# When GpSimd computes its low halves and powers, and when the row maxima and LayerNorm 2 are transposed, in a fused attention and FFN layer

## The reference

```python
x = x + attention(layernorm(x), W_qkv, W_out)
x = x + ffn(layernorm(x), U1, V1, b1, U2, V2, b2)

# attention: 32 query heads, 16 key/value heads (each shared by 2 query heads), head size 64
scores = q @ k.T / 8 + slope[head] * (key - query); causal mask; softmax; @ v; @ W_out
# ffn, rank 64:  gelu_tanh((x @ U1) @ V1 + b1) -> @ U2 -> @ V2 + b2
# layernorm: (x - mean) / sqrt(var + 1e-5)
```

## Time and profile before

| | |
|---|---|
| time, median of 3 runs | 2876.21 us (2874.03 to 2881.04) |
| profiled execution: time / span | 2881.05 us / 2879.3 us |
| mean granted clock of PE | 0.989 |
| busy, share of the span | PE 93%, ACT 76%, POOL 70%, DVE 69% |
| a MID body | 173.7 us |
| chain that ended last | PE 71%, ACT 8%, DVE 7%, issue 7%, POOL 5%, DMA 1% |

### The profile page before, as it was taken

How to read it: one execution, slowest core, us unless ns; L and a number is a source line. 1 busy time by engine, 2 the same in 40 slices (tenths; PEclk the granted TensorE clock), 3 DMA queues, 4 the chain that set the end, 5 groups by cost and what they waited for, 6 DMA issues and landing times.

```text
span 2879.3 us, 83610 instructions
## 1 busy us (share of the span) xinstructions
PE 2680.9 (93%) x31112; PEld 1834.4 (64%) x31112; DVE 1992.4 (69%) x6731; ACT 2184.7 (76%) x3892; POOL 2011.7 (70%) x1816
## 2 busy tenths in 40 slices
PE   4999999999999999999999999999999999999986
PEld 1566666766666666666766667666666766667663
DVE  6767676776766767676776776767677676767753
ACT  3777878778787777878778787777878778787782
POOL 1667777777777767777677777777777677777783
PEclk8999999999999999999999999999999999999996
DMA  6444443444434344343544434344343444435420
GB/s 170 96 100 88 94 90 79 104 91 91 89 87 99 82 97 88 87 97 78 105 90 93 89 84 101 85 94 87 88 99 81 98 91 91 92 77 105 87 61 20
DMA packets 495146, 260.82 MB, mean 91 GB/s; under 512 B 317962, under 2 KB 493066, under 8 KB 494474
## 3 DMA queue, kind: packets, MB, share of 16 engines
q1 hardware_dynamic: 494740, 255.47, 40.8%
HBM read 27.73 MB, written 8.39 MB: 13 GB/s over the span
## 4 chain that ended last, share of the span: by engine, by line
PE 71%; ACT 8%; DVE 7%; issue 7%; POOL 5%; DMA 1%; SPq 0%; DVEq 0%; ACTq 0%; POOLq 0%
PE proj L450 31%; PE scores L450 17%; PE o_acc L450 13%; PE max_scores L450 4%; PE ffn_acc L450 4%; ACT h_f L830 2%; POOL p_lo L1090 2%; DVE max_scores L930 2%; ACT p_hi L700 2%; POOL o_hi_lo L1098 2%; ACT p_f L741 2%; ACT L741 1%; DVE h_hi L1022 1%; DMA o_t<-in_L_attn_W_out 1%; POOL h_lo L1118 1%
## 5 line engine op out<-in xcount | busy, mean ns | idle before, releaser
L1090 POOL TENSOR_TENSOR p_lo<-p_f,p_hi 128x512 f16<-128x512 f32 x1280 | 1474.4, 1159 | 564.6 <-ACT p_hi L700 564.4
L741 ACT ACTIVATE p_f<-scores 128x512 f32<-128x512 f32 x1280 | 755.6, 590 | 130.0 <-PE scores L450 126.2
L700 ACT ACTIVATE p_hi<-p_f 128x512 f16<-128x512 f32 x1280 | 800.4, 625 | 14.8
L930 DVE CUSTOM_DVE_ANT_0 max_scores<-max_scores,causal 128x384 f32<-128x384 f32 (+3 forms) x1184 | 563.3, 507 | 268.7 <-PE max_scores L450 257.7
L450 PE MATMUL scores<-q_hi_lo,k_lo_hi 128*128 128x512 f16 (+3 forms) x2048 | 614.2, 300 | 0.2 <-ACT p_f L741 0.2
L450 PE MATMUL scores<-q_hi_aug,k_hi_aug 128*128 128x512 f16 (+3 forms) x2048 | 586.5, 299 | 0.0
L450 PE MATMUL o_acc<-v_hi_one,p_lo 128*128 128x65 f16 x5120 | 518.9, 195 | 42.9 <-POOL p_lo L1090 39.9
L450 PEld LDWEIGHTS o_acc<-v_hi_one,p_lo 128*128 128x128 f16 x5120 | 471.1, 98 | 90.7 <-POOL p_lo L1090 63.2
L450 PE MATMUL o_acc<-v_hi_one,p_hi 128*128 128x65 f16 x5120 | 518.3, 194 | 0.0
L450 PE MATMUL o_acc<-v_lo,p_hi 128*128 128x64 f16 x5120 | 517.9, 193 | 0.0
L450 PEld LDWEIGHTS o_acc<-v_lo,p_hi 128*128 128x128 f16 x5120 | 468.7, 99 | 37.8
(11 more groups left out here) (108 smaller groups left out, 4680.8 us busy)
## 6 DMA issues: line engine op xcount, KB each, us to landing
q_hi_aug<-q_pair_hi SPq DMA_DIRECT2D x512, 64.0 KB, 2.0
q_hi_lo<-q_pair_hi SPq DMA_DIRECT2D x512, 64.0 KB, 2.0
q_hi_lo<-q_pair_lo SPq DMA_DIRECT2D x512, 64.0 KB, 2.0
k_hi_aug<-k_pair_hi SPq DMA_DIRECT2D x256, 64.0 KB, 2.0
k_lo_hi<-k_pair_hi SPq DMA_DIRECT2D x256, 64.0 KB, 2.0
k_lo_hi<-k_pair_lo SPq DMA_DIRECT2D x256, 64.0 KB, 2.0
x_rows<-in_L_attn_inputs SPq DMA_DIRECT2D x17, 512.0 KB, 4.0
x_acc<-in_L_attn_inputs SPq DMA_DIRECT2D x64, 128.0 KB, 2.3
```

The costliest lines, as they stand in the source:

```text
L700: return nc.scalar.activation(out_ap, in_ap, ACT.Copy, scale=scale)
L741: nc.scalar.activation(p_f[:, k % 3, :], score_bank[k % 2][:, :], ACT.Exp).then_inc(exp_done, 1)
L930: last = nc.vector.tensor_tensor_reduce(out=bank, in0=bank, in1=causal[:, (T - 1 - qt) * P:S], scale=1.0, scalar=-3e38, op0=ALU.add, op1=A ...
L1090: nc.gpsimd.tensor_tensor(p_lo[:, slot, n, :], p_f[:, k % 3, :], p_hi[:, slot, n, :], ALU.subtract).then_inc(lo_p, 1)
```

## The change

It moves instructions and adds or removes none of the computation:

- POOL: `low_p` of the stage before now stands ahead of `o_lo` at the start of every stage. `power1` moves from the end of stage 7 to (8, 2), behind that segment's `low_p`. LayerNorm 2's powers move from (8..11, 4) to (9..12, 0), behind `low_p` and `o_lo`.
- The maxima are transposed in segment 2 of stages 2, 6, 10 and 14, not in segment 1. ACT's and DVE's splits of them follow the same table.
- LayerNorm 2: normalising goes from segment 1 to 2, transposing from 2 to 3 of stages 9 to 12. On PE the transposes now stand behind `attend(s, 1)`. DVE's low half of the transposed tile moves to segment 3 with them, and on DVE it stands ahead of that segment's `normalise`.
- DVE's `neg_mean_rstd` goes from (8, 2) to (8, 4).
- `projection_order()` reads the same tables, so the banks of all uses between these places rotate differently.

```diff
-MAX_SEG, K_SEG, V_SEG, O_SEG = 1, 0, 4, 4
+MAX_SEG, K_SEG, V_SEG, O_SEG = 2, 0, 4, 4
...
-VE1_AT, NMR1_AT = (7, 4), (8, 2)
+VE1_AT, RS1_AT, NMR1_AT = (7, 4), (8, 2), (8, 4)
...
-RSTD2_AT = {(8 + t, 4): t for t in range(T)}
-LN2_AT = {(9 + t, 1): t for t in range(T)}
-LN2_T_AT = {(9 + t, 2): t for t in range(T)}
+RSTD2_AT = {(9 + t, 0): t for t in range(T)}
+LN2_AT = {(9 + t, 2): t for t in range(T)}
+LN2_T_AT = {(9 + t, 3): t for t in range(T)}
...
-                            if (s, n) in LN2_T_AT:
-                                transpose_x2(LN2_T_AT[s, n])
...
                         if n in (1, 3) and in_stage(mode, s, ATT + 1):
                             attend(s, n // 2)
+                        if (s, n) in LN2_T_AT and mode != FIRST:
+                            transpose_x2(LN2_T_AT[s, n])
...
+                        if n > 0 and in_stage(mode, s, ATT):
+                            low_p(SEG * (i * KV + s - ATT) + n - 1, s % 2, n - 1, SEG * s + n - 1)
+                        if n == 0 and in_stage(mode, s, ATT + 1):
+                            low_p(SEG * (i * KV + s - ATT) - 1, (s - 1) % 2, SEG - 1, (SEG * s - 1) % (SEG * KV))
                         if n == 0 and in_stage(mode, s, ATT + 2):
                             slot = (s - ATT - 2) % 2
                             pool.wait_ge(hi_o, at(i * KV + s - ATT - 1))
                             nc.gpsimd.tensor_tensor(o_hl[:, slot, 1, :], o_f[:, slot, :, :].rearrange("p t c -> p (t c)"),
                                                     o_hl[:, slot, 0, :], ALU.subtract).then_inc(lo_o, 1)
-                        if n > 0 and in_stage(mode, s, ATT):
-                            low_p(SEG * (i * KV + s - ATT) + n - 1, s % 2, n - 1, SEG * s + n - 1)
-                        if n == 0 and in_stage(mode, s, ATT + 1):
-                            low_p(SEG * (i * KV + s - ATT) - 1, (s - 1) % 2, SEG - 1, (SEG * s - 1) % (SEG * KV))
+                        if (s, n) == RS1_AT and mode != LAST:
+                            power1(i + 1)
...
-                    if s == 7 and mode != LAST:
-                        power1(i + 1)
```

## The result

The changed kernel takes 2882.95 us (median of 13 runs, 2881.08 to 2887.88), the kernel before beside it 2878.0 us (13 runs, 2874.03 to 2881.04). The ratio is 1.0022, interval 1.0013 to 1.0030: 5 to 6 us slower, less than the 0.3% that I called measurable, but clear of 1 by its interval. I had forecast 7 us faster.

What follows compares the result with a forecast made beforehand. PE, busy 93% of the span, bounds the kernel, so its waits are lost time. Gains of 44 and 4.6 us against losses of 39 and 2 us gave about -7 us: 2869 us from 2876.2, range 2838 to 2895.

Steps and rivals of the forecast that it cites:

- The four gains of a MID body: PE waits removed in stages 8, 9, 10 and 2: 1.22, 0.67, 0.82 and 0.22 us, 44 us over 15 bodies.
- k copies at (6, 0) and (8, 0), 0.8 each: Stages 5 and 7: later `o_lo` delays SP's k copies past PE's need, 1.6 us a body together.
- Stages 1 and 3, 0.15 each: k copies behind `o_lo` on SP, late only where an issue or landing is slow: 0.15 us in each stage.
- What is added: Cost step: later `o_lo` holds SP's queue and maxima land later, 2.6 us a body, 39 us, and 2 us once.
- Maxima in segment 2: Stage 6's maxima have nothing in hand before (7, 0): 0.4 us a body; stages 10 and 14 have more in hand.
- the `o_t` transposes: Those needed by output projections of stages 4 and 12, delayed behind later `o_lo` on SP: 0.1 us each.
- FIRST, 2 us: Scores of (7, 0) in the FIRST body wait for the maxima's transpose, now behind a q projection: 2 us, once.
- LAST, 4.6 us: `o_lo` leaves the chain, POOL's work of 6.95 us then limits: 0.65 us a stage over about 7 stages gained.
- A: Rival: only the gains, since SP's copies are not late; 2829 us, chance 0.15.
- B: Rival: SP's queue takes more than is won, at k copies before (6, 0) and (8, 0); 2895 us, chance 0.18.
- C: Rival: `x2n` waits for POOL at the shared port pair, 0.8 us a body in stage 10; 2881 us, chance 0.06.
- D: Rival: ACT's late `p_hi` keeps `attend` waiting in stages 8 and 9, gain about 1 us; 2883 us, chance 0.06.

Runs made afterwards that it cites:

- Experiments one: Kernel before with only `o_lo` moved behind `low_p` on GpSimd; powers, banks and transposes unmoved: 2895.0 us, ratio 1.0053.
- two: Kernel before with only both kinds of LayerNorm powers moved, behind `o_lo`, which stays ahead of `low_p`: 2843.2 us, ratio 0.9882.
- three: Kernel before with only the maxima transposed in segment 2 and LayerNorm 2's subtraction and transpose one segment later: 2873.6 us, ratio 0.9984.
- Experiment four: Changed kernel with `o_lo` back ahead of `low_p`, all else as changed: 2842.0 us, ratio 0.9875.
- experiment five: Changed kernel with the 512 KB load of the next batch's rows issued in stage 2, not stage 1 (`X_LOAD = 2`): 2884.6 us, ratio 1.0019.
- experiment seven: Changed kernel with `o_lo` ahead of `low_p` in FIRST and MID bodies, behind it in LAST alone: 2835.4 us, ratio 0.9852.
- the mended order: SP issues even stages' `o_t` transpose behind the next stage's k copies: on the changed kernel 2856.9 us, on the good one 2826.8 us.
- the good one: Changed kernel with `o_lo` behind `low_p` in LAST alone and stage 6's maxima transposed in segment 1: 2822.1 us, ratio 0.9811.

## Why the prediction was wrong, step by step

*The four gains of a MID body* were right in place and a little small: 1.22 was 1.36 and 0.67 was 0.89 (a segment gained some 0.2 us more than its wait's row shows; why, I haven't tried); 0.82 and 0.22 were won in full, with 0.28 more for the transpose that left these segments, part of it paid back a segment later. Net 3.6 us where I had 2.93. But I gave the gain of stages 8 and 9 to the power and `o_lo` as one block, 1.22 and 0.67, and didn't ask which of the two had to go. Experiments one and two say: either. With the powers gone `o_lo` ends in time for `p_lo` to follow, so `o_lo` could have stayed.

*k copies at (6, 0) and (8, 0), 0.8 each:* 0.45 and 1.03, together 1.48 for 1.6. Right. The forecast that `o_t` of stage 5 starts 3.2 us after the stage's first scores came out at 737.87 - 734.85 = 3.0. *Stages 1 and 3, 0.15 each:* 0.33 and 0.06. The shift of the first k copy was 2.8 us by my sum; in stage 1 it was 3.0 (from 2.83 to 5.84 after the first scores, mean), in stage 3, where I had read it, 2.2.

*Maxima for (7, 0), 0.4:* 0.31. Right.

*What failed* is the step "What is added", in its list of what is queued behind `o_lo` on SP: "the `o_t` transpose, and in odd stages the k rows and six k copies". It leaves out stage 2. There SP issues a 512 KB load that no other stage has, and behind it the copies of the maxima for (3, 0). I gave this nothing, and it cost 0.73 us a body, 11 us, the largest term without a price and alone more than the 7 us that I forecast as gain. The later step "Maxima in segment 2" names every stage of the four but this one. What it does say of stages 10 and 14 came out right: in the changed kernel their second copy still lands 2.1 and 4.1 us before the scores. Before, stage 2's copies land 3.0 us ahead of (3, 0) on average. In the changed kernel SP issues them straight behind the load, and they take 3.6 us to land (2.5 before) and not the 2.0 of the earlier trace rows, which is the landing of another line. Experiments one, three, four and five show that it is queue and load, not the segment: one has the loss with `MAX_SEG` at 1, three and four don't have it with `MAX_SEG` at 2, and five takes it away by moving the load.

*Second, the `o_t` transposes.* I gave (4, 4) and (12, 4) 0.1 each and (8, 4) nothing; they cost 0.45, 0.11 and 0.28. I had looked for who is queued behind `o_lo` on SP, and taken the k copies since they are the last in the queue; but `o_t` itself is the first. At stage 4 its own reader had 3.1 us in hand (mean), and the transpose of stage 3 starts 3.3 us later. At stage 8 the reader had 2.1 us in hand, and two things took them: the transpose starts 1.1 us later after (8, 0), and (8, 1) before the reader became 1.36 us shorter, by the very gain that I had forecast. Experiment four has 0.24 of this wait without a late `o_lo`.

*The sum.* Losses of 3.8 us a body for 2.6, gains of 3.6 for 2.93: +0.24 for -0.33, a difference of 8.6 us over 15 bodies. The losses are 1.15 over mine: 0.73 in stage 2 and 0.64 for `o_t`, less 0.2 by which the others came out smaller. The larger gains hid 0.7 of it, which was luck. Between the profiles the forecast missed by 8 us (-7.6 for +0.3); the rest of the 13 is that the profiled execution before lay 3.0 us above its kernel's median and the one after 1.6 below. *FIRST, 2 us:* 2.25, but not where I put it. Its first scores start at 76.17 for 76.14; the loss is at (10, 0) and (12, 0), where k copies are late by 1.6 and 1.9 us and some gains are behind them. Over all fourteen profiles the first scores start at 75.3 us on average with the maxima of stage 6 in segment 1 (seven kernels, 73.9 to 76.8) and at 76.4 with them in segment 2 (seven, 75.7 to 77.5): some 1.1 us of the 2 seem real, which one start alone can't tell. *LAST, 4.6 us:* 3.9 to the last scores, and 4.5 with its end in experiment seven. The period is 6.88 us. The chain of the changed kernel's LAST body (start, length, what), to compare with the earlier trace rows:

```profile
2800.59 1.16 POOL p_lo L1090
...
2806.77 0.63 ACT p_hi L700
...
2807.47 1.17 POOL p_lo L1090
```

The length is right within 0.07, its reason isn't: I took POOL's own work as the limit, the chain still goes from POOL to PE, DVE and ACT and back.

*The rivals.* A (only the gains, 2829) is what the changed kernel does once `o_lo` is put back, nearly: 2842, or 2835 with `o_lo` late in LAST alone. B (SP's queue takes more than is won) is the side on which it fell, by the mechanism given but at other places than its two: it decided from 0.5 us a body over my sum, and the losses were 1.2 over it, half of that made good by the gains. My sign for it was DMA waits above 50 us, and the three rows "issue", `o_t` and `q_hi_aug` come to 51.7. C (the port pair) didn't come: `x2n` in the changed kernel, iteration 4, DVE, with GpSimd beside it at the third tile:

```profile
799.68 2.27 POOL L1090 TENSOR_TENSOR p_lo<-p_f,p_hi 128x512 f16<-128x512 f32 x2
800.97 1.13 DVE L964 TENSOR_SCALAR h_f<-x_rows,bn_aggr,rstd 128x256 f32<-128x256 f32 x1
```

It takes 0.48, 0.57, 1.13 and 0.59 us on average for the four tiles, 2.8 us in all for 2.5 before. The rule of the Trainium skill ("SBUF — State Buffer", Who interferes with whom), by which the one that starts first holds the other off for its whole instruction, fits only in part: the second `p_lo` ends at 801.95, and held off until then `x2n` would have ended at 802.36, 0.41 later, where it ended at 802.10. No PE wait for it follows in stage 10, where the rival put its 0.8 us. D (`attend` not freed) didn't come either: no MID body has a wait for `p_lo`.

*My range* held the time, and the direction was wrong by 13 us on terms that each were of the order of 40: a difference of two sums that I knew to 20 us could not carry a sign, and I gave it one.

## What to carry to other kernels

When an edit takes several instructions out of a wait, ask which of them suffices, and price the others' delay as a cost of their own: here the powers gave all 33 us, and `o_lo`, moved with them, added nothing in the MID bodies and cost 41. When an instruction is made later, follow the queue that waits for it through every stage, not through the two with the tightest margin: list for each stage what is issued behind it, the first item as well as the last, with its own landing time at that place. A queue's order has a value only where the queue is late: the mended order that won 26 us in the late kernel won nothing in the good one.

## What the runs showed that I had not expected

- A small copy (8 KB, from a tile of 32x128 to one row) took 3.6 us to land when a 512 KB load was issued on the queue straight ahead of it, 2.5 us when it was issued 0.7 to 1.6 us after the load's issue had ended (before), 2.0 us without the load (experiment five) and 1.9 us when the load was some 3 us ahead (experiments three and four), each over all MID bodies. The load's own landing went from 4.0 us before to 4.5 (medians). The Trainium skill ("SBUF — State Buffer", The DMA setup-cost knee) gives every transfer a roughly fixed 2 us that doesn't scale with its size. The usual 1.9 to 2.0 agree; the 3.6 show that what was issued just ahead counts as well.
- The edits don't add: alone they are +16, -35 and -5 us, together +5. Two of them win the same 2.2 us a body, which can be won only once. Of the third's new waits those for `p_lo` at (7, 1) and (11, 1), 0.29 and 0.32 us, are gone in the changed kernel.
- Once waits for DMAs are on the path, two kernels with the same code there differ by 4 us over 15 bodies; stages 0, 1, 3 and 5, which have none, keep their mean lengths within 0.01 us in all fourteen kernels.
